# The second accumulator joined to the first behind block 66, and output rows made ahead of the next bias forms

## The reference

```python
vals, idx = jax.lax.top_k(logits, TOP_K)                     # TOP_K = 4
gates_k = jax.nn.softmax(vals, axis=-1)
h = jnp.einsum('mh,eoh->emo', t, w1) + b1[:, None, :]
a = jnp.minimum(h[..., ::2], LIMIT)
b = jnp.clip(h[..., 1::2], -LIMIT, LIMIT)
act = a * jax.nn.sigmoid(ALPHA * a) * (b + 1.0)
y = jnp.einsum('emi,edi->emd', act, w2) + b2[:, None, :]
delta = jnp.einsum('me,emd->md', G, y)                       # G: the gates, zero for experts not chosen
```

## Time and profile before

| | us |
|---|---|
| median of 3 runs (range) | 1005.02 (1004.24 to 1008.51) |
| the profiled execution, device time | 1002.58 |
| its span in the trace | 1000.8 |

### The profile page before, as it was taken

One profiled execution on the slowest core, in us unless ns is written; L12 is line 12 of the kernel. 1 busy time (PEld: TensorE's weight loads), 2 busy tenths in 40 slices (PEclk: granted clock), 3 DMA queues, 4 the chain that ended last, 5 costly groups with the idle time before them and its releaser, 6 DMA issues. The chain is left out here.

```text
span 1000.8 us, 20579 instructions
## 1 busy us (share of the span) xinstructions
PE 969.1 (97%) x6073; PEld 819.3 (82%) x6073; DVE 716.9 (72%) x2499; ACT 673.2 (67%) x1944; POOL 435.2 (43%) x455
## 2 busy tenths in 40 slices
PE   9999999999999999999999999999989989999993
PEld 5769878987887887788789888888768779999992
DVE  4464657767677687768776866785788877888883
ACT  3657778587758757866785776687565647766771
POOL 2322421331263164237225513624137775556876
PEclk9999999999999999999999999999999999999997
DMA  9946993899499421012002001427339789999983
GB/s 316 303 134 219 377 377 125 289 376 376 159 330 376 166 87 54 2 55 87 1 17 104 23 1 41 160 79 270 133 74 249 194 242 254 231 226 235 251 222 63
DMA packets 95517, 182.12 MB, mean 182 GB/s; under 512 B 10237, under 2 KB 30141, under 8 KB 94797
## 3 DMA queue, kind: packets, MB, share of 16 engines
q1 hardware_dynamic: 75243, 149.64, 44.6%
q0 software_dynamic: 18720, 30.79, 13.7%
q10 hardware_dynamic: 1442, 0.38, 0.2%
HBM read 78.22 MB, written 109.56 MB: 188 GB/s over the span
## 5 line engine op out<-in xcount | busy, mean ns | idle before, releaser
L2042 POOL TENSOR_TENSOR RB<-RB 128x512 f32<-128x512 f32 x64 | 66.9, 1045 | 259.4 <-DVE RB L1824 259.3
L1222 PE MATMUL bank<-RB 128*128 128x128 f32 x1264 | 157.1, 276 | 1.8 <-DVE BC L1938 0.7
L1222 PEld LDWEIGHTS bank<-RB 128*128 128x128 f32 x1264 | 149.5, 192 | 4.5 <-DVE BC L1938 1.1
L1505 ACT ACTIVATE RB<-RA,nw 128x512 f32 x158 | 105.4, 714 | 46.8 <-issue 19.8
L1184 PE MATMUL bank<-RA,RB 128*128 128x256 f32 x512 | 133.0, 382 | 2.0 <-ACT RB L1406 2.0
L1156 PE MATMUL bank<-RA 128*128 128x256 f32 x512 | 121.3, 380 | 0.0
L1156 PEld LDWEIGHTS bank<-RA 128*128 128x128 f32 x512 | 95.0, 190 | 15.0 <-issue 3.2
L1184 PEld LDWEIGHTS bank<-RA,RB 128*128 128x128 f32 x512 | 91.2, 190 | 15.9 <-issue 3.0
L2018 POOL TENSOR_TENSOR qs<-qs,half 128x4 f32<-128x4 f32 x64 | 65.5, 1023 | 62.9 <-DVE qs L1833 49.7
L1243 PE MATMUL bank<-RB,BC 128*128 128x256 f32 x316 | 82.0, 383 | 3.2 <-DVE BC L1951 2.8
L1406 ACT ACTIVATE RB<-bank 128x256 f32<-128x256 f32 x128 | 48.6, 380 | 47.8 <-PE bank L1175 46.7
(11 more groups left out here) (263 smaller groups left out, 2394.7 us busy)
## 6 DMA issues: line engine op xcount, KB each, us to landing
xsD<-BC SPq DMA_DIRECT2D x17, 4232.0 KB, 32.8
RB<-in_w2b SPq DMA_DIRECT2D x79, 256.0 KB, 3.8
RB<-xsD SPq DMA_DIRECT2D x68, 264.5 KB, 4.1
BC<-modD SPq DMA_DIRECT2D x16, 512.0 KB, 4.0
RA<-in_w SPq DMA_DIRECT2D x10, 512.0 KB, 6.3
X<-xsD SPq DMA_DIRECT2D x11, 264.5 KB, 3.1
RA<-in_L_attn_Wq SPq DMA_DIRECT2D x2, 1024.0 KB, 10.4
RA<-in_L_attn_Wo SPq DMA_DIRECT2D x1, 2048.0 KB, 17.3
```

The lines of the kernel that those rows point to most:

```text
L1222: m = pe.matmul(ps[:, 128 * j:128 * j + 128], WS[:, n % 2, c, 128 * j:128 * j + 128], XT[:, n % 2, c * 128:c * 128 + 128], start=(c == 0), ...
L1505: m = act.activation(WS[:, n % 2, c, :], W1[:, bass.ds(r, 1), c, :].rearrange("p a n -> p (a n)"), ACT.Copy, scale=nw[:, c:c + 1])
L2042: pool.tensor_tensor(sq, qrow, qrow, ALU.mult).then_inc(mine("q_sq", p), 1)
```

## The change

It does two things, both in the second stretch only.

First, the accumulators. `ACC2` is used for blocks 55, 58, 61 and 64 only. Behind the `y_add` of block 66, one merge adds all of `accE` (rows 1280 to 2047, 768 KB) to `accD`. It keeps the name `merge(ACC2, 7)` and waits for the landings of `y_add(64)` and `y_add(65)`. Blocks 66 and 67 go to `OUT`, and from 68 on the even blocks go to `ACC` and the odd ones to `OUT`. `y_add` of block 68 and of the later `ACC` blocks waits for that merge. The merges of `ACC` 0 to 4 stand behind 57, 58, 60, 62 and 64, those of `ACC` 5 and 6 behind 70 and 73, and `ACC` 7 stays last. `merge(ACC2, 5)` and `merge(ACC2, 6)` are gone, so nine merges are left. SyncE's closing waits are on the `ACC` merges alone.

Second, the order in a turn: `y_out(n-3)` now stands ahead of `e_a(n)`, not behind `e_b(n)`.

```diff
-THREE, TWO = blocks_with_rows_below(PART), blocks_with_rows_below(NB - 1)
-ADDED_TO = [n % 2 for n in range(THREE)] + [(ACC2, ACC, OUT)[(n - THREE) % 3] for n in range(THREE, TWO)] + [ACC, OUT, OUT, ACC, OUT, ACC, OUT, ACC]
-MERGE_BEHIND = {57: (ACC, 0), 59: (ACC, 1), 61: (ACC, 2), 63: (ACC, 3), 65: (ACC, 4), 66: (ACC, 5), 68: (ACC2, 5),
-                72: (ACC2, 7), 74: (ACC, 6), 76: (ACC2, 6)}
+THREE = blocks_with_rows_below(PART)
+JOIN = 66
+ADDED_TO = [n % 2 for n in range(THREE)] + [(ACC2, ACC, OUT)[(n - THREE) % 3] for n in range(THREE, JOIN + 1)] + [OUT] + [(ACC, OUT)[n % 2] for n in range(JOIN + 2, NBLK)]
+MERGE_BEHIND = {57: (ACC, 0), 58: (ACC, 1), 60: (ACC, 2), 62: (ACC, 3), 64: (ACC, 4), JOIN: (ACC2, NB - 1), 70: (ACC, 5), 73: (ACC, 6)}
...
+        if lo <= n - 3 < hi:
+            p.add("y_out", n - 3, bank=5 + n % 3, last=True)
+        if lo <= n < hi:
             p.add("e_a", n, bank=bk)
             p.add("e_tanh", n)
             p.add("e_b", n, bank=bk, last=True)
         if lo <= n - 3 < hi:
-            p.add("y_out", n - 3, bank=5 + n % 3, last=True)
             p.add("y_add", n - 3, slot=ADDED_TO[n - 3], by=16)
...
-                if ADDED_TO[n] == ACC and n > TWO + 1:
+                if ADDED_TO[n] == ACC and n > JOIN:
                     on.wait_ge(*done("merge", ACC2, NB - 1))
...
-                final = blocks_with_rows_below(max(b + 1, PART))
-                target = OUT
-                if (acc, b) == (ACC2, NB - 1):
-                    target, final = ACC, TWO + 1
-                elif acc == ACC2:
-                    on.wait_ge(*done("merge", ACC, b))
-                elif b == NB - 1:
-                    on.wait_ge(*done("merge", ACC2, b))
+                target, final, rows = OUT, blocks_with_rows_below(max(b + 1, PART)), slice(256 * b, 256 * b + 256)
+                if acc == ACC2:
+                    target, final, rows = ACC, JOIN + 1, slice(256 * PART, 2048)
+                elif b >= PART:
+                    on.wait_ge(*done("merge", ACC2, NB - 1))
```

More of the change, by code:

```diff
@@ L959, in _ @@
             for b in range(NB):
-                on.wait_ge(*done("merge", ACC2 if b in (5, 6) else ACC, b))
+                on.wait_ge(*done("merge", ACC, b))
         @block.tensor
@@ L2110, in merge @@
             def merge(acc, b):
-                final = blocks_with_rows_below(max(b + 1, PART))
-                target = OUT
-                if (acc, b) == (ACC2, NB - 1):
-                    target, final = ACC, TWO + 1
-                elif acc == ACC2:
-                    on.wait_ge(*done("merge", ACC, b))
-                elif b == NB - 1:
-                    on.wait_ge(*done("merge", ACC2, b))
+                target, final, rows = OUT, blocks_with_rows_below(max(b + 1, PART)), slice(256 * b, 256 * b + 256)
[3 more added lines that the diff above has]
+                    on.wait_ge(*done("merge", ACC2, NB - 1))
                 on.wait_ge(*done("y_add", last_added(acc, final)))
                 on.wait_ge(*done("y_add", last_added(target, final)))
-                to_, of = (a[256 * b:256 * b + 256, :].rearrange("(a c) n -> a (c n)", c=8) for a in ((out_r, accD)[target], (None, accD, accE)[acc]))
+                to_, of = (a[rows, :].rearrange("(a c) n -> a (c n)", c=8) for a in ((out_r, accD)[target], (None, accD, accE)[acc]))
                 pool.dma_start(to_, of, accum_op=ALU.add, max_dma_last_dim=8192).then_inc(mine("merge", acc, b), 16)
```

## The result

The changed kernel takes 1008.24 us (median of 16 runs, 1005.66 to 1011.34) against 1005.61 us for the kernel before (16 runs, 1004.22 to 1008.51). The ratio is 1.0029, 95% interval 1.0018 to 1.0039. The medians differ by 2.6 us and the ratio stands for 2.9 us; either way it is slower, where 1.4 us faster was forecast. Its profiled execution took 1008.84 us, with a span of 1007.1.

The account below looks back on a forecast made before the run. TensorE was taken to bound 920 to 960, GpSimd's queue of additions the tail. Join landing at 970.0 plus 21.7 gave 991.7 against 993.09, so -1.4 us: 1003.6 from 1005.02, range 1000.0 to 1008.1.

Parts of the forecast that it names:

- the old join: In the tail, block 74's addition waits for merge(ACC2, 7), issued at 977.77 and 4.8 us to landing.
- when the join is issued: On GpSimd behind block 66's addition: issued at 959.5, when block 65's addition has landed.
- The addition of 65 near 953.8: On GpSimd: from 956.08 to near 953.8, with rows 2.0 us earlier and the merge behind it gone.
- Its landing in 5.2 to 6.2 us: Block 65's addition lands 5.2 (median) to 6.2 us after it begins, at about 959.5.
- The transfer of 768 KB in 10.5 us: The new join takes 6.3 plus twice 2.1 us, putting its landing and block 68's addition at 970.0.
- the low bound: Shortest time for the 768 KB join: 4.1 us with 1.7 of transfer in it, twice more of these, 7.5.
- 21.7 us from 68 to 78: GpSimd's backlog: seven paces of 2.01, two with a merge of 2.83, one of 1.96; last addition at 991.7.
- the join lands late: Rival: a join over 11.9 us makes the kernel slower, up to +3.1; chance 0.15, shared with paired landings.
- The floor of -4.2: In the tail: block 78's addition could begin at 988.9 at the earliest against 993.09, 4.2 us sooner.
- The rival on paired landings: From 68 on, same-accumulator landings, 5.2 us per two blocks, replace GpSimd's pace: slower by 3; 0.15 with late join.
- The cover of 3 us for a waiting y_out: Between e_act(n) and y_mm(n), two turns later on TensorE, 3 us are free before a waiting y_out costs.
- The rival was nearer: Rival: the big transfer delays weight loads beyond 5.2 us to spare, TensorE stops, end +1 to +3 us; chance 0.05.

Follow-up runs that it names:

- e6: The changed kernel without the five merges of accD into out for sequences 0 to 4, their sums left out of the output: ratio 0.9993 against the kernel before.
- e8: The kernel before, unedited, profiled once more: device time 1005.0 us.
- e5: The changed kernel with a join of only accE's last 256 rows, 256 KB in place of 768: ratio 1.0013 against the kernel before.
- e3: The changed kernel without the join and the waits for it, sums of blocks 55, 58, 61 and 64 left out: ratio 1.0003 against the kernel before.
- e11: The changed kernel with the join one place later, behind the addition of block 67: ratio 1.0075 against the kernel before.
- e4: The changed kernel with y_out(n-3) between e_a(n) and e_b(n), behind e_tanh(n): ratio 1.0037 against the kernel before.
- e1: The kernel before with only y_out moved ahead of e_a, its accumulators and merges kept: ratio 0.9996 against the kernel before.
- e12: The changed kernel with the merges of ACC 1 to 4 behind 59, 61, 63 and 65: ratio 1.0016 against the kernel before.

## Why the prediction was wrong

The path was right: the tail is GpSimd's queue, the old join started its backlog, and the time goes with the addition of 68 plus the paces. What fell is one term, **when the join is issued**: 959.5 in the prediction, 967.50 in the trace, which is 964.5 on the scale above, so 5.0 us late. Step by step, on the scale above:

- *The addition of 65 near 953.8.* It came at 960.42, which is 957.4 on the time of the earlier trace rows: 3.6 us late. "Its rows come 2.0 us earlier" held, but the addition does not follow its rows. They were there at 955.2, and GpSimd came to them 5.2 us later without being idle for more than 0.17 us at any addition behind that of 62:

```profile
954.76 0.48 DVE L1961 SCALAR_TENSOR_TENSOR BC<-bank,RB 128x256 f32<-128x256 f32 x1
```
```profile
952.43 1.58 POOL L2109 DMA_INDIRECT accD<-BC,to  x1 [0.89 <-DVE X L1961]
...
955.27 1.64 POOL L2109 DMA_INDIRECT out<-RB,to  x1 [0.17 <-issue]
...
957.45 1.71 POOL L2109 DMA_INDIRECT accE<-X,to  x1 [0.16 <-DVE RB L1948]
958.59 1.46 POOL L2122 DMA_DIRECT2D out<-accD  x1
```

  Ahead of 62 it was held by landings (the additions of 58 and 59 took 8.0 us each, and 61 and 62 waited for them), from there by its own queue. "The merge behind it is gone" was a misreading: that merge now stands behind 64, straight ahead of the addition of 65. e6, without the five merges, has 65 where I put it (-28.2); in the twelve traces with these merges and the third accumulator, both kernels included, it is at -22.7 to -25.6, wherever y_out and the small merges stand. The first profile, from which I took 956.08, has the earliest of these (-25.6; -24.2 in e8), so 1.4 of the 3.6 us can be scatter of that one trace.
- *Its landing in 5.2 to 6.2 us.* It took 6.6, and the join followed it by 7.1: 1.4 us more than the 5.7 used. The rows cited for 6.2 go up to 7.3.
- *The transfer of 768 KB in 10.5 us.* It was 8.65 us from issue to the addition of 68, 1.85 less. The guess by bounds was on the safe side. The 1.7 us of transfer in the low bound stand in no row of before; from e5 and the changed kernel it is 1.8 us per 256 KB, and the low bound (7.5) was the near one.
- *21.7 us from 68 to 78.* It was 22.8, 1.1 more: some pairs wait for a landing (the addition of 70 begins at 981.47, 5.3 behind that of 68).
- The sum: -1.4 + 3.6 + 1.4 - 1.85 + 1.1 = +2.85 us, against +2.9 in the trace. It must come out so, since its terms are the pieces of one trace; it says where the 4.3 us between forecast and trace lie, namely 5.0 in the issue of the join.

The rival "the join lands late" named the right outcome and the right turning point (the addition of 68 at 971.4; it was at 973.2 on that scale), but for the wrong reason: I let only the length of the transfer vary and kept the time of its issue fixed at 959.5. With that bound open, the late case would have been given more than 0.15. The prediction's own sign of being wrong, a last addition behind 995, came: 996.0 on that scale. The range ended at 1008.1, 0.1 us short of the median.

*The floor of -4.2* was mis-sized. Without any join the last addition is at +9.6 (e3), 1.8 us earlier than before, because two accumulators are paced by landings of 5.2 us. The rival on paired landings had that mechanism and that figure, but put it behind block 68, where landings took 2.7 to 4.5 us in the changed kernel and no pace of pairs set in; in e3 it works from 66 to 71.

*The cover of 3 us for a waiting y_out* was wrong. I counted from e_act to y_mm and left out that ScalarE is behind e_a too. In the changed kernel ScalarE's tanh, and w_in and x_out of the next turn, stand in one queue:

```profile
977.96 0.42 ACT L1520 ACTIVATE BC<-RB 128x256 f32<-128x256 f32 x1 [2.11 <-DVE RB L1933]
978.59 1.33 ACT L1507 ACTIVATE RB<-RA,nw 128x512 f32 x2 [0.22 <-PE bank L1224]
979.83 0.36 ACT L1514 ACTIVATE RB<-bank 128x256 f32<-128x256 f32 x1
```
```profile
980.34 2.02 PE L1224 MATMUL bank<-RB 128*128 128x128 f32 x16 [0.69 <-ACT RB L1514]
```

The tanh comes 2.11 us late, and TensorE waits for the x_out behind it. The cover is about 1 us (e11). Here it did not set the end (e4).

*The rest held.* y_out moved for nothing by itself (e1), and it begins 0.98 us ahead of its turn's e_a in place of 1.24 behind it, so the rows came 2.2 us earlier against that e_a (2.0 forecast). TensorE was full from 920 to 960. Loads did not stop TensorE: its waits there are for ScalarE. The rival was nearer than that sounds, though. The weights issued 1.2 us behind the join (968.71) took 7.6 us to landing, where the weights issued from 960 to 980 in the kernel before took 4.5 at most:

```profile
RB<-in_w2b SPq DMA_DIRECT2D x1, 256.0 KB, 7.6
```

That is 3.1 us of the 5.2 to spare. Ahead of the join too, from 925 on, weights took up to 8.7 us in the changed kernel (5.7 before), and TensorE did not wait for them. The Trainium skill (DMA: Bandwidth & Descriptors, section Anatomy of one DMA) gives about 2.0 us plus the bytes over 436 GB/s, by which the join would take 3.8 us as an estimate; the trace has 7.8 us to landing, and the measurement decides.

## What to carry to other kernels

When an operation is moved ahead, ask not only when its input is ready but what its own queue is doing at that time: for a chain of additions that must land one after the other, the issuing engine's queue and the landings set the issue time, and work put into it elsewhere (five merges, issued 9 to 29 us ahead of the join) moves it. Where a term of a sum is a wait for a landing, let the issue vary as well as the length before a range is drawn. And the slack of an instruction is the least over every engine that waits for it, so follow each queue behind it, not only the one that leads to the bottleneck by the obvious way.

## What the runs showed of the hardware

- An accumulating transfer from memory to memory grew slowly with its size: 5.1 us from issue to release of the next for 256 KB (e5), 8.65 us for 768 KB at the same place, so 1.8 us per further 256 KB. Over all merges of the kernel before, 256 KB each, the median to landing was 6.3 us.
- An addition of 128 rows took 2.7 us to land at the least and 8.0 us in the changed kernel behind a merge (block 58) and behind the join (block 67). That a merge stands right behind it too makes no difference that can be seen: without that merge block 58 took about as long (e12). The issue rows of those two, with microseconds to landing last:

```profile
accE<-RB,to POOLq DMA_INDIRECT x1, 8.0
```
```profile
out<-BC,to POOLq DMA_INDIRECT x1, 8.0
```

- Two executions of one kernel differed by 2.3 us in where block 78 began, with the distance from there to the last addition equal to 0.05 us, and with the distances from the additions of 65 and 68 to it different by 1.4 and 1.5 us. A comparison of two single traces by absolute time would have put that on the change.
